# Exponentials of two PSUM banks as one ScalarE operation in an attention and mixture-of-experts kernel

## The reference

```python
x = L0_attn_x                       # (2, 2048, 256) float32
xn = layernorm(x)
# attention: 16 heads of 16, K and V projected from xn, with relative positions
scores = einsum('bhld,bhrd->bhlr', Q, K) * scale + einsum('bhld,lrd->bhlr', Q, rel_k)
attn = softmax(scores, axis=-1)
out = einsum('bhlr,bhrd->bhld', attn, V) + einsum('bhlr,lrd->bhld', attn, rel_v)
# feed-forward: 8 experts, the 2 best per token, silu(gate) * up, then down
x = x + (out @ Wo.T + bo) + experts(xn)
```

## Time and profile before

| | |
|---|---|
| median of 3 runs | 3461.26 us (3460.48 to 3466.33) |
| profiled execution, first to last instruction | 3463.7 us, the only time that its page gives |
| PE busy | 3194.2 us (92%) |
| PEld busy | 2524.8 us (73%) |
| DVE busy | 2813.3 us (81%) |
| ACT busy | 2634.6 us (76%) |
| POOL busy | 2262.5 us (65%) |
| exponentials (L1077) | 2048 of 688 ns on average, 1313.5 us busy, 305.7 us idle before them |
| low parts on GpSimd (L850) | 1984, 1857.7 us busy, 583.8 us idle before them |

### The profile page before, as it was taken

The page is one execution under the profiler, slowest core; times in us unless marked ns, Lnnn a source line. Parts: engine busy times, 40 slices in busy tenths (PEclk is TensorE's granted clock), DMA queues, the critical chain, the costliest instruction groups (busy, mean ns, idle before and its releaser), DMA issues. The chain is left out here.

```text
span 3463.7 us, 165894 instructions
## 1 busy us (share of the span) xinstructions
PE 3194.2 (92%) x64918; PEld 2524.8 (73%) x64918; DVE 2813.3 (81%) x7853; ACT 2634.6 (76%) x5852; POOL 2262.5 (65%) x2526
## 2 busy tenths in 40 slices
PE   7589999999999999999999999999999996999990
PEld 4357777777777777777777777777777785579980
DVE  6479999999999999999999999999999986534443
ACT  3288888888888888888888888888888893234440
POOL 0167777777777777777777777777777774700006
PEclk9779999999999999999999999999999997589995
DMA  7776666666666666666666666666666664712224
GB/s 212 228 230 216 221 220 221 221 221 224 218 221 224 221 223 224 222 218 224 221 223 224 223 217 221 224 224 221 224 218 222 222 217 161 239 51 69 62 62 145
DMA packets 356374, 701.28 MB, mean 202 GB/s; under 512 B 59545, under 2 KB 168706, under 8 KB 355346
## 3 DMA queue, kind: packets, MB, share of 16 engines
q1 hardware_dynamic: 349458, 673.92, 60.3%
q0 software_dynamic: 6144, 16.79, 1.5%
HBM read 343.02 MB, written 347.46 MB: 199 GB/s over the span
## 5 line engine op out<-in xcount | busy, mean ns | idle before, releaser
L850 POOL TENSOR_TENSOR pt_near<-pt_full,pt_near 128x512 f16<-128x512 f32 (+3 forms) x1984 | 1857.7, 965 | 583.8 <-DVE pt_near L1170 583.8
L1077 ACT ACTIVATE pt_full<-pb,exp_bias 128x512 f32<-128x512 f32 x2048 | 1313.5, 688 | 305.7 <-PE pb L960 183.9
L1011 PEld LDWEIGHTS pb<-pt_near,table_high 128*128 128x128 f16 x18432 | 794.6, 97 | 145.1 <-issue 106.4
L1011 PE MATMUL pb<-pt_near,table_high 128*128 128x64 f16 (+6 forms) x18432 | 884.8, 187 | 15.7 <-DVE rel_out L1203 14.6
L1150 DVE TENSOR_REDUCE part_max<-pb 128x1 f32<-128x512 f32 (+3 forms) x1376 | 771.2, 574 | 131.0 <-PE pb L918 130.0
L1011 PE MATMUL pb<-pt_near,table_low 128*128 128x64 f16 (+6 forms) x9216 | 851.4, 187 | 0.0
L1011 PEld LDWEIGHTS pb<-pt_near,table_low 128*128 128x128 f16 x9216 | 772.7, 97 | 0.0
L1146 DVE CUSTOM_DVE_ANT_0 near_sum<-pb,skewed 128x512 bf16<-128x512 f32 (+3 forms) x1216 | 675.6, 571 | 109.4 <-PE pb L918 85.0
L952 PE MATMUL pb<-ident,skewed 128*128 128x128 f32 x3840 | 621.6, 285 | 20.5 <-ACT q_max L1101 19.2
L1170 DVE CAST pt_near<-pt_full 128x512 f16<-128x512 f32 (+3 forms) x1280 | 532.3, 466 | 0.3 <-PE pb L984 0.3
L984 PE MATMUL pb<-v_head,pt_near 128*128 128x33 f16 x13440 | 507.2, 178 | 9.1 <-POOL pt_near L850 5.5
(11 more groups left out here) (182 smaller groups left out, 4063.3 us busy)
## 6 DMA issues: line engine op xcount, KB each, us to landing
skewed<-rel_scratch SPq DMA_DIRECT2D x256, 576.0 KB, 5.3
rel_scratch<-rel SPq DMA_DIRECT2D x416, 319.5 KB, 3.4
rel_scratch<-rel SPq DMA_DIRECT2D x320, 320.0 KB, 2.8
skewed<-rel_scratch SPq DMA_DIRECT2D x64, 512.0 KB, 4.6
skewed<-rel_scratch SPq DMA_DIRECT2D x64, 448.0 KB, 4.3
k_stack<-planes_scratch SPq DMA_DIRECT2D x192, 96.0 KB, 4.7
planes_scratch<-planes SPq DMA_DIRECT2D x64, 256.0 KB, 2.3
rel_scratch<-rel SPq DMA_DIRECT2D x64, 256.0 KB, 2.7
```

Of the source, the lines that this page charges most:

```text
L850: ins = nc.gpsimd.tensor_tensor(pt_piece(c, 1, a, z, near), pt_full[e][:, (a - 4 * g) * P:(z - 4 * g) * P], pt_piece(c, 0, a, z, near), AL ...
L1011: ins = nc.tensor.matmul(acc[:, c0:c1, :], keep[table][:, w:w + P], pt_near[half][:, part, c0:c1, d - M_LO, a * SHIFTS:(a + 1) * SHIFTS], ...
L1077: nc.scalar.activation(pt_full[e][:, :], x_ps[e % 2][:, :], ACT.Exp, bias=exp_bias[:, 0:1]).then_inc(s_exp, 1)
```

## The change

The four SBUF tensors `pt_full[e]` become two tensors of two parts each, and the two PSUM banks `x_ps` become one tensor `turned_ps` of two banks. The banks keep their places. ScalarE does the exponentials of a pair as one operation over 2 x 512 elements. It waits for both turned-score semaphores and for the low parts of both parts of the unit before, and its semaphore `s_exp` counts pairs. TensorE waits, before it writes a pair's banks, for the whole pair before it. The high parts wait for their pair.

```diff
-        pt_full = [sb(f"pt_full{i}", [P, CH]) for i in range(E)]
+        pt_pair = [sb(f"pt_full{i}", [P, E // 2, CH]) for i in range(E // 2)]
+        pt_full = [pt_pair[e // 2][:, e % 2, :] for e in range(E)]
...
-        psum = [ctx.enter_context(nc.psum_tensor(f"pb{i}", [P, CH], FP32)) for i in range(8)]
-        score_ps, x_ps, r_ps = psum[:BANKS], psum[BANKS:BANKS + 2], psum[7]
-        o_ps = psum[6][:, 0:HALF_C * VW]
+        score_ps = [ctx.enter_context(nc.psum_tensor(f"pb{i}", [P, CH], FP32)) for i in range(BANKS)]
+        turned_ps = ctx.enter_context(nc.psum_tensor("pb_turned", [P, E // 2, CH], FP32))
+        x_ps = [turned_ps[:, i, :] for i in range(E // 2)]
+        sums_ps = ctx.enter_context(nc.psum_tensor("pb_sums", [P, CH], FP32))
+        r_ps = ctx.enter_context(nc.psum_tensor("pb_rel", [P, CH], FP32))
+        o_ps = sums_ps[:, 0:HALF_C * VW]
...
-                        pe.wait_ge(s_exp, it * (4 * STEP) + 4 * u + e - 1)
+                        pe.wait_ge(s_exp, 2 * u + pair)
...
-            def exponentials(it, u, e):
-
-                act.wait_ge(s_x[e % 2], it * (2 * STEP) + 2 * u + e // 2 + 1)
+            def exponentials(it, u, pair):
+
+                for s in s_x:
+                    act.wait_ge(s, 2 * u + pair + 1)
                 if u >= 1:
 
-                    wait_low(act, it, u - 1, e)
-                nc.scalar.activation(pt_full[e][:, :], x_ps[e % 2][:, :], ACT.Exp, bias=exp_bias[:, 0:1]).then_inc(s_exp, 1)
+                    for e in (2 * pair, 2 * pair + 1):
+                        wait_low(act, it, u - 1, e)
+                nc.scalar.activation(pt_pair[pair][:, :, :], turned_ps[:, :, :], ACT.Exp,
+                                     bias=exp_bias[:, 0:1]).then_inc(s_exp, 1)
...
-                act.wait_ge(s_exp, it * (4 * STEP) + 4 * u + e + 1)
+                act.wait_ge(s_exp, 2 * u + e // 2 + 1)
...
                     exponentials(it, k - LAG_X, 0)
-                    exponentials(it, k - LAG_X, 1)
...
-                    exponentials(it, k - LAG_X, 2)
-                    exponentials(it, k - LAG_X, 3)
+                    exponentials(it, k - LAG_X, 1)
...
-                dve.wait_ge(s_exp, it * (4 * STEP) + 4 * u + e + 1)
+                dve.wait_ge(s_exp, 2 * u + e // 2 + 1)
```

## The result

| | before | after |
|---|---|---|
| median | 3462.98 us (3460.48 to 3466.33, 4 runs) | 3496.86 us (3494.65 to 3498.22, 4 runs) |
| ratio | | 1.0095, 95% interval 1.0080 to 1.0109 |
| span of the profiled execution | 3463.7 us | 3495.0 us (its run took 3496.76) |

The change makes the kernel slower by 0.95%, 34 us. The forecast was slower by 58 us (3519), in a range from 3480 to 3565, which holds the result.

What follows compares the result with a forecast made beforehand. It took TensorE to wait on ScalarE at c = 9 to 15, with GpSimd pacing c = 4 to 7. A loss of 1.8 us x 32 heads = 58 us on the 3461.3 us median gave 3519 us, range 3480 to 3565.

Steps and rivals of the forecast that it cites:

- What bounds the kernel: At c = 9 to 15 (c: a unit's place among a head's 16), TensorE waits about 0.10 us per unit on ScalarE.
- The operation: ScalarE's exponentials of a pair: 1.11 us joined against 1.26 for two, saving 0.15 us per pair, of 1024 pairs.
- The joint wait costs more than the operation saves: First pair waits for GpSimd's second low part, idling TensorE 0.8 us at c = 8, 0.1 to 0.3 at six other units.
- c = 8 term: TensorE's second half at c = 8 comes at 1.53 us instead of 0.74 after the exponentials start: 0.79 us late.
- What the saving buys: Earlier query rows give TensorE back 0.10 us at c = 10 to 15 and 0, some 0.06 at 3 and 4.
- The walk: TensorE's lateness followed unit by unit through one head: 0.79 us at c = 8, 1.45 at c = 3, then 1.8 at the end.
- I take 1.8: At the end of c = 4 to 7 a head is 1.8 us late, chosen between 1.26 and 2.25.
- a low part is as late as TensorE was: GpSimd's low part is delayed as much as TensorE was at its own unit's first half, making GpSimd 1.26 us late from c = 2.
- C: Rival: joined operation takes 1.27 us, saving nothing; some 2.1 us more per head, 125 us in all, 3586; chance 0.08 with worse.
- A: Rival: the late low part never binds, only the second pair's saving counts; 0.97 us per head, 31 us faster, 3430; chance 0.11.
- B: Rival: no change, 3461 us; only the 0.79 us at c = 8 counts and 0.82 comes back; chance 0.06.
- D's lower case: Rival: another ring in c = 4 to 7, 1.26 us instead of 1.8, 3502 us; chance 0.75 together with the forecast.

Runs made afterwards that it cites:

- the fastest run: Kernel before with only the second pair as one operation, waiting on one turned-score semaphore carried by the operation, its own semaphore raised by one: 3440.06 us, ratio 0.9932.

## Why the prediction was right in direction and too large

*What bounds the kernel.* Right for c = 9 to 15: TensorE waited on ScalarE's query rows by 0.10 us per unit while it looked busy (a gap of 0.13 before, 0.03 in the fastest run). That GpSimd paces c = 4 to 7 fits all runs too, though none changed its work.

*The operation.* 1.115 us against 1.11 forecast. The figure from the Trainium skill (ScalarE: Activation LUTs, What ACT_TABLE_LOAD costs) gave 1.13; the measurement decides for 1.115.

*The joint wait costs more than the operation saves.* Right, and shown from three sides: taken away by a second set, the loss vanishes (1.0095 to 1.0002); put alone on the kernel before, the joint wait loses as much (1.0105); with the first pair alone as one operation it is all there (1.0106), with the second alone there is none in all (0.9995).

*The long hold of the banks.* The prediction had it inside its c = 8 term and did not part it from the late low part. With a second set TensorE idles 0.41 us there, with one 0.75; so somewhat over half of the wait is the hold, the rest the low part. It costs the kernel little: with two sets, 3442.49 us with the first pair as one operation and 3440.59 with it as two.

*What the saving buys.* The step was mis-sized on two counts. The prediction had 0.10 us per unit, the changed kernel got 0.07, since its pair starts 0.117 us behind the products and not 0.03. "Exponentials wait for four semaphores ahead of one operation; the early ones are passed while the operation before runs" costed this at nothing. That is so for the early ones, but the one that comes last stood in the instruction ahead of the operation (0.05 us), and the later of two products counts (0.03 us).

*The walk.* Its sum failed in the last stretch. "I take 1.8" let a head end between GpSimd's lateness of 1.26 us and TensorE's 2.25. The runs show that it ends at GpSimd's own: 0.82 us at c = 4, and 0.79 for the head. TensorE was 1.40 late there, and what it had beyond GpSimd went into its waits at c = 7: -0.61 us in the stretch where the walk has +0.35. And GpSimd itself was less late than 1.26. One reason is a second idea, "a low part is as late as TensorE was", that everyone is delayed by the same amount. It holds where nobody else holds TensorE up, and from c = 10 to c = 2 each step came out within about 0.1 us; at c = 9 it doesn't, where VectorE held TensorE up in most heads, and 0.41 us came back by medians, 0.27 by means, where the walk has 0.10 for another reason. Against that c = 3 lost 0.2 more than the walk had, where the pair waited for VectorE's part 3, and GpSimd didn't feel it.

*Luck.* Per head the forecast was 1.8 us and the loss 0.8, a factor of over two. The kernel's time is nearer, 58 us against 34, because the first head alone lost 5.2 us, which no term of the walk explains. The upper end of the range doesn't come out of its own words either: half of C's further loss gives 3552 us and not 3565.

*The rivals.* A, faster by 31 us, has its premise in the runs with two sets, where the low parts don't bind. The first of them gained nothing (3462.73), since the pairs started late; with one wait less 18 to 21 of the 31 us came (3445.56 and 3442.49). The rule of the Trainium skill that an unsaturated ScalarE should have its instructions broken up (Perfetto Trace Analysis, Optimizing Scalar/DVE Operations) fits the first pair. Its other rule, that grouping can help where the engine is saturated, wouldn't have found the second: grouping it on an engine that idles paid 23 us (3463.4 to 3440.06), because that pair stands on the ring between TensorE's products and its next transposes. C is out by the duration. B is out, as what came back didn't cover the delays. D's lower case, GpSimd's 1.26 us and 3502 us, was the nearest: it has the right mechanism, with too late a GpSimd.

*Left open.* Why the first head loses 5.2 us, why the second set costs 0.3 us at c = 7, with or without the long operation, and what makes the race at c = 8 between VectorE and GpSimd come out one way or the other.

## What to carry to other kernels

Joining two operations joins their waits: before doing it, look up for each wait how long after the first operation's start it is satisfied, and compare that with the slack of whoever comes next. Join where the operation lies on the ring and its waits are early in most units (here the second pair, -0.68%), and leave it split where the later input comes in between. When a delay is carried through several units, look for a stretch in which another engine works without a break: what leaves it is that engine's lateness, and whatever the first had beyond it is given back in its waits. Follow more than one period, as two that look alike can differ in a wait. And put the wait that comes last on the operation itself, not on an instruction ahead of it.

## What the runs showed of the hardware

An exponential over 2 x 512 elements across two PSUM banks took 1.115 us against 0.688 for 512: 0.83 ns per element more. Copies within one bank grow by 0.84, so no price of the second bank is seen. The place of a wait is worth tens of nanoseconds: the operation started 0.117 us after TensorE's last product with the late semaphore in the instruction ahead, 0.083 with it on the operation and an early one ahead, 0.068 with no other wait left for the scores, and 0.19 when the operation raised its semaphore by two and carried no wait. Across a whole kernel the order of two lines was worth 4 to 5 us by the medians.

VectorE's high parts (float32 to float16, SBUF to SBUF) and GpSimd's operations held each other up. Of the 1280 high parts on VectorE in the kernel before, 312 start while a GpSimd operation runs; 299 of these take longer than the same size elsewhere and end mostly 0.08 to 0.29 us behind the end of GpSimd's operation. Of the other 968 none takes longer. At c = 6 this makes 2.50 us of three high parts of 0.42, 0.22 and 0.35.
